# A second buffer for the tile of new node features, in the third and fourth node stages of a four-layer graph network

## The chip, the cores and the metric

The kernel runs on one core of one Trainium2 chip. The time is the device time of one execution, in microseconds (us); several executions are timed and their median is given.

## What is computed

A graph of 6250 nodes with 128 features each and 100,000 edges, sorted by destination, goes through four layers. Each layer's result is added to its input and normalised:

```python
x = _layernorm(x + L0(x, src, dst))                      # gated differences over the edges
x = _layernorm(x + L1(x, src, dst, edge_weight))         # attention with 4 heads, each normalised
x = _layernorm(x + L2(x, edges, edge_attr_32))           # attention with 8 heads, then
                                                         #   x1 = _layer_norm(x + agg @ Wo + bo)
                                                         #   _layer_norm(x1 + gelu(x1 @ W1 + b1) @ W2 + b2)
x = _layernorm(x + L3(x, edges))                         # two attention layers with 4 heads
```

In L1 the sum over a node's edges is divided by its denominator, every head is normalised over its 32 features (`norm_feat`) and averaged with the same of the node's own projection. The attention layers need a softmax over the edges that enter a node, so every layer gathers a row per edge, weighs it, and sums by destination.

## The kernel before, in words

The nodes lie on 128 partitions in 49 blocks (NB), and a node stage works through them in KG = 7 groups of KB = 7 blocks, so one pass over a group is 128 x 896 elements. The program alternates: node stage `ph` (0 to 5) builds new features of all nodes and the tables for the next edge loop; edge loop `ph` (0 to 4) gathers table rows for 56 groups of edges and leaves sums by destination in DRAM; the next node stage gathers those. Stage `ph` = 2 is the third node stage, `ph` = 3 the fourth. All order between engines is written out by hand with semaphores; each engine runs its own list of instructions in order. `link` and `tell` issue one DVE instruction and wait for it, so DVE has one pass in flight at a time, and many of its operations carry the line of a helper: L1281 is `tensor_tensor`, L1285 `tensor_scalar`, L1289 a copy, L1292 `scalar_tensor_tensor`, L1295 a reduction.

**Third stage.** DVE runs `features(0)`, then for each g `features(g+1)` and `tables(g)`. `features(g)` (L1849) takes the gathered sums of group g, divides, normalises each head (`norm`, L1593), scales, adds the kept own part `aux` and the old features X, all in the tile `t1` (a part of `rows`, called f1 there; f2 is scratch), and takes the statistics (`centre`, L1576). It has asked ACT for two square roots on the way (L1075). ACT then centres the seven blocks of t1 (L1088, semaphore n_x), PE turns them (L741, n_t), ACT copies the turned tile from PSUM to xT (L1064, L1065, n_xT) and copies t1 into X (L1144, n_kept); PE multiplies xT with the weights (L910, L913, n_mm). `tables(g)` (L1909) adds biases in three passes from PSUM (L1281) and counts n_stage. SyncE (SP) then saves the table (L550, L552), and GpSimd (POOL) scatters the rows of the group to the edges (`spread_rows`, L660). POOL also gathers the sums for the groups to come (`gather_sums`, L652); its list holds the gathers of three groups, then a gather and a scatter by turns. Before it writes t1, `features` waits for the turn and for the copy into X of the group before it (L1854 to L1857).

**Fourth stage.** A group passes through `head` (divide, into t1), `project` on PE (turn t1, multiply with Wo), `inner` on DVE (add X, statistics, in x1s[g % 2]), the feed-forward part on PE and ACT (turn x1 at L741, matrices at L870, gelu at L1159, second matrices at L882, n_ff2), `outer_first` on DVE (L1804: x1 times a gain into the tile yq, plus the second product from PSUM, statistics, a reciprocal root by three Newton steps on DVE, scaling), `outer_second` (L1831: gain, bias, plus X, statistics), ACT's centring of yq (L1088, y_ready), PE's `table_rows` (turn yq, matrices at L857 and L858), ACT's `keep` (L1146: copy to xT, copy yq into X at L1149, n_kept), and `tables`. DVE's round in this stage is outer_first(k-1), tables(k-2), outer_second(k-1), inner(k+1), head(k+2) (L1971 to L1981). PE's is: turn x1 of group k, L870, project(k+1), the second matrices, table_rows(k-1) (L864 to L885). `project(k)` waits from k = 3 on for the count that `tables(k-3)` gives. ACT's is: copy of the turned x1, eight gelus, copy for the projection, root and centring of outer_second(k-1), of inner(k+1), keep(k-1) (L1154 to L1168). The wait in question is the second line of `outer_first`, L1807: `dve.wait_ge(n_kept, kp.value())`, the copy of the group before.

yq is a part of `rows` (L157); `msg` (L94) is a tile of its own that DVE uses as scratch (f3) in the second node stage only, for the tables of that stage, and between edge loops for 132 columns.

## Time and profile before

| | us |
|---|---|
| three runs | 6608.78, 6615.19, 6615.32 |
| median | 6615.19 |
| the profiled execution | 6610.64 |
| its span, first to last instruction | 6608.9 |
| third node stage, about | 172 |
| fourth node stage, about | 245 |

The profile is of one execution, by the hardware's profiler. Engines are PE (TensorE), DVE (VectorE), ACT (ScalarE), POOL (GpSimd) and SP (SyncE); PEld is PE's load of weights. Over the whole span DVE is busy for 4656.9 us (70%), POOL for 4285.6 (65%), ACT for 1375.1 (21%) and PE for 1263.0 (19%). In a line of the timeline stand the start, the duration, the engine, the line of the code, the operation, what it writes and reads, the shapes and the count; in brackets the idle time of the engine before it and what ended that. Lines of the timeline can merge several instructions (x3).

### The profile page before, as it was taken

To read this page: it belongs to the slowest core of one execution; us is meant where nothing else is said; L and a number is where in the kernel's file an instruction comes from. 1 tells how busy PE (TensorE), PEld (TensorE's weight loads), DVE (VectorE), ACT (ScalarE), POOL (GpSimd) and SP (SyncE) were. 2 spreads that over 40 slices of the span, in tenths; PEclk is the share of its full clock that TensorE was granted. 3 is DMA by queue.
4 is the path that set the end of the run, shared out by engine and by line. 5 is a ranking of instruction groups with operands and counts; after the bars stand their busy time and mean duration, and the time that the engine had idled before them with its cause. 6 is when DMAs were issued, how large, how long until landed. Compare 5 with 4: busy or idle time off the path is not lost. (4 is left out here: it accounts for less than half of the span.)

```text
span 6608.9 us, 37159 instructions
## 1 busy us (share of the span) xinstructions
PE 1263.0 (19%) x8049; PEld 1103.2 (17%) x8049; DVE 4656.9 (70%) x9455; ACT 1375.1 (21%) x3580; POOL 4285.6 (65%) x4445
## 2 busy tenths in 40 slices
PE   7100000245555533332000000810000010000000
PEld 6100000135455433322000000610000010000000
DVE  7788888799999969976888887644444444444445
ACT  0122222221111114421000000622222211222223
POOL 1777777657777760026777775357777767777775
PEclk9555555555555555556555555855555555555555
DMA  9666666334444437744666664123333323333332
GB/s 386 208 213 202 202 203 203 123 105 132 136 134 135 133 130 295 294 155 139 218 224 215 224 218 157 29 75 112 111 109 115 109 79 91 109 115 109 110 113 82
DMA packets 338944, 1032.97 MB, mean 156 GB/s; under 512 B 100325, under 2 KB 163137, under 8 KB 331294
## 3 DMA queue, kind: packets, MB, share of 16 engines
q0 software_dynamic: 166752, 401.68, 21.3%
q1 hardware_dynamic: 116642, 342.34, 14.8%
q10 hardware_dynamic: 55324, 286.57, 12.0%
q8 instruction: 63, 1.03, 0.1%
q14 instruction: 163, 1.34, 0.1%
HBM read 602.97 MB, written 427.39 MB: 156 GB/s over the span
## 5 line engine op out<-in xcount | busy, mean ns | idle before, releaser
L722 POOL DMA_INDIRECT rows<-table,idx x3136 | 2988.0, 953 | 985.1 <-issue 972.9
L641 POOL DMA_INDIRECT by_src<-ebuf,place x784 | 764.9, 976 | 275.6 <-issue 239.0
L1292 DVE SCALAR_TENSOR_TENSOR psA<-psA,cont,dstf 128x128 f32<-128x128 f32 (+1 forms) x2349 | 836.6, 356 | 45.5 <-ACT ebuf L1021 24.8
L1281 DVE TENSOR_TENSOR sc<-rows,ebuf 128x56 f32<-128x56 f32 x112 | 28.2, 252 | 1023.6 <-DMA rows<-table,idx 1023.6
L954 PE MATMUL psA<-dstf,ones 128*128 128x512 f32 x10 | 9.9, 1114 | 3056.3 <-DVE dstf L2213 3056.3
L1292 DVE SCALAR_TENSOR_TENSOR sums<-sums,cont,psA 128x128 f32<-128x128 f32 (+1 forms) x1512 | 519.4, 344 | 30.2 <-ACT psA L1217 29.0
L954 PEld LDWEIGHTS psA<-dstf,ones 128*128 128x128 f32 x10 | 2.7, 316 | 3057.9 <-issue 3057.9
L820 PE MATMUL psA<-attr,sums 128*128 128x49 f32 x1568 | 406.1, 404 | 468.6 <-DVE attr L1471 468.6
L2094 DVE TENSOR_TENSOR_SCAN psA<-rows,psA 128x1980 f32<-128x1980 f32 x112 | 480.1, 4287 | 3.9
L820 PEld LDWEIGHTS psA<-attr,sums 128*128 128x128 f32 x1568 | 397.0, 327 | 474.7 <-DVE attr L1471 474.7
L1223 ACT ACTIVATE psA<-df 128x60 f32<-128x60 f32 (+1 forms) x168 | 40.4, 241 | 1716.0 <-DVE df L1281 1716.0
L1281 DVE TENSOR_TENSOR psA<-rows,psA 128x1848 f32<-128x1848 f32 (+1 forms) x168 | 352.9, 2101 | 0.0
L729 POOL DMA_INDIRECT fixr<-states,fixi x5 | 5.0, 997 | 518.3 <-DMA states<-sums 464.6
L660 POOL DMA_INDIRECT spread_wide<-rows,nidx x147 | 154.7, 1052 | 244.9 <-DMA spread_wide<-sums 143.9
L1281 DVE TENSOR_TENSOR rows<-rows,psA 128x1792 bf16<-128x1792 bf16 (+3 forms) x121 | 234.4, 1937 | 109.2 <-DMA rows<-table,idx 105.6
L652 POOL DMA_INDIRECT sums<-states,nidx x245 | 255.8, 1044 | 81.0 <-issue 73.1
L1238 ACT ACTIVATE sums<-psA 128x1848 f32<-128x1848 f32 x112 | 191.5, 1710 | 460.0 <-DVE psA L2094 460.0
L1281 DVE TENSOR_TENSOR rows<-psA,rows 128x1792 f32<-128x1792 f32 (+2 forms) x168 | 203.3, 1211 | 118.3 <-DMA rows<-table,idx 106.7
L1019 ACT ACTIVATE ebuf<-psA 128x1792 f32<-128x1792 f32 x56 | 94.2, 1681 | 902.4 <-DMA by_src<-ebuf,place 782.6
L792 PE MATMUL psA<-ebuf 128*128 128x49 bf16 x588 | 63.6, 276 | 963.4 <-DVE ebuf L1281 963.4
L1217 ACT ACTIVATE psA<-rows,wt 128x128 f32<-128x128 f32 x784 | 233.0, 352 | 33.8 <-DVE wt L2114 33.8
L792 PEld LDWEIGHTS psA<-ebuf 128*128 128x128 bf16 x588 | 54.5, 144 | 972.4 <-DVE ebuf L1281 972.4
(337 smaller groups left out, 5556.0 us busy)
## 6 DMA issues: line engine op xcount, KB each, us to landing
dstf<-spread_wide SPq DMA_DIRECT2D x168, 924.0 KB
states<-sums ACTq DMA_DIRECT2D x150, 952.0 KB, 4.0
rows<-by_src SPq DMA_DIRECT2D x55, 1035.0 KB, 5.1
states<-sums ACTq DMA_DIRECT2D x56, 1008.0 KB, 5.9
spread_wide<-sums SPq DMA_DIRECT2D x56, 924.0 KB, 24.7
states<-sums ACTq DMA_DIRECT2D x56, 903.0 KB, 7.3
rows<-table,idx POOLq DMA_INDIRECT x3136
msg<-low_rows SPq DMA_DIRECT2D x56, 448.0 KB, 3.7
```

The costliest lines, as they stand in the source:

```text
L641: pool.indirect_dma_start(by_src[:, :], bass.IndirectOffsetOnAxis(ap=place[:, s, j:j + 1], axis=0), payload[:, s, j, :], None).then_inc(so ...
L652: pool.indirect_dma_start(nrows[g % NS][:, b * w:(b + 1) * w], None, states[ph - 1][:, :], bass.IndirectOffsetOnAxis(ap=nidx[:, order, k:k ...
L660: pool.indirect_dma_start(spread[ph][:, :], bass.IndirectOffsetOnAxis(ap=nidx[:, 1, k:k + 1], axis=0), zslot(ph, g)[:, b * ZW[ph]:(b + 1) ...
L722: pool.indirect_dma_start(rows[:, at:at + GW[ph]], None, table[ph][:, :], bass.IndirectOffsetOnAxis(ap=idx[:, s, j:j + 1], axis=0)).then_i ...
L792: m = pe.matmul(cells, hotS[:, :, j], hotSH[:, :, j], start=False, stop=True, skip_group_check=True)
L820: pe.matmul(t, hotT[s][:, j, :], cell[:, :, j], start=True, stop=False)
L1019: act.activation(payload[:, s, :, 0:ROW].rearrange("p b (h d) -> p b h d", d=33)[:, :, :, 0:32], heldS[:, :, 0:D].rearrange("p b (h d) -> ...
L1217: m = act.activation(gated[:, j * D:(j + 1) * D], rows[:, at:at + D], ACT.Copy, scale=wt[:, s, j:j + 1])
L1238: act.activation(S3[:, :, 0:F], chain_msg.rearrange("p (f b) -> p b f", b=B + 1)[:, 1:B + 1, :], ACT.Copy).then_inc(states_turned, 1)
L1281: return dve.tensor_tensor(o_, a_, b_, op)
L1292: return dve.scalar_tensor_tensor(o_, a_, s_, b_, op0, op1)
L2094: tell(dve.tensor_tensor_scan(chain_msg, chain_gate, chain_msg, 0.0, ALU.mult, ALU.add), su)
```

## The change

In the third stage groups of even number are built in t1 as before, those of odd number in f3, a view of `msg`; in the fourth the same with yq and f3. Every reader follows: DVE's passes, ACT's centring and its copy into X, PE's turn. The waits of DVE in front of a group's first write are moved back by one group: in the third stage group 1 has none, and group g from 2 on waits for the turn and the copy of group g - 2; in the fourth `outer_first(g)` waits for the copy of group g - 2. A local name in `outer_first` is changed to make room (y becomes r), which alters no instruction; those lines are left out.

```diff
--- before.py
+++ after.py
@@ -156,6 +156,9 @@
         x1s = [t2, rows[:, o:o + KB * P].rearrange("p (b d) -> p b d", d=P)]
         yq = rows[:, o + KB * P:o + 2 * KB * P].rearrange("p (b d) -> p b d", d=P)
         mixed = [t1, yq]
+        f3 = msg[:, 0:KB * D].rearrange("p (b d) -> p b d", d=D)
+        fresh = [t1[:, :, 0:D], f3]
+        yqs = [yq, f3]
         dflat = dstf[:, :, :, :].rearrange("p s b d -> p (s b d)")
         hT = dflat[:, 0:4 * KB * P].rearrange("p (c n) -> p c n", c=4)
         sflat = small[:, :, :].rearrange("p a b -> p (a b)")
@@ -848,7 +851,7 @@
 
                 def table_rows(k):
 
-                    turn_x(yq, y_ready, k + 1)
+                    turn_x(yqs[k % 2], y_ready, k + 1)
                     if k < KG - 2:
                         pe.wait_ge(proj_read, k + 3)
                     if k:
@@ -898,7 +901,8 @@
                     if ph:
                         x.add()
                         pe.wait_ge(n_x, x.value())
-                    turn(KB, lambda b: t1[:, b, 0:D] if ph else X[:, g * KB + b, :]).then_inc(n_t, 1)
+                    entry = fresh[g % 2] if ph == 2 else t1
+                    turn(KB, lambda b: entry[:, b, 0:D] if ph else X[:, g * KB + b, :]).then_inc(n_t, 1)
                     xt.add()
                     pe.wait_ge(n_xT, xt.value())
                     w = 256 if ph < 3 else 136
@@ -1096,7 +1100,7 @@
                 def outer_second(k):
 
                     root(1, KB, 0)
-                    centre(2 * KG + 2 * k + 2 - int(k == KG - 1), yq, y_ready)
+                    centre(2 * KG + 2 * k + 2 - int(k == KG - 1), yqs[k % 2], y_ready)
 
                 def evict(g):
 
@@ -1125,7 +1129,7 @@
                     if ph == 2:
                         root(1, 28, 1)
                         root(1, KB, 0)
-                        centre(KG + g, t1, n_x)
+                        centre(KG + g, fresh[g % 2], n_x)
                     if ph == 4:
                         turned(ACT.Relu)
                         if g < KG - 1:
@@ -1141,12 +1145,12 @@
                     if ph in (0, 1, 2):
                         turned()
                     if ph in (1, 2):
-                        act.activation(X[:, grp(g), :], t1[:, :, 0:D], ACT.Copy).then_inc(n_kept, 1)
+                        act.activation(X[:, grp(g), :], fresh[g % 2] if ph == 2 else t1[:, :, 0:D], ACT.Copy).then_inc(n_kept, 1)
 
                 def keep(g):
 
                     turned()
-                    act.activation(X[:, grp(g), :], yq, ACT.Copy).then_inc(n_kept, 1)
+                    act.activation(X[:, grp(g), :], yqs[g % 2], ACT.Copy).then_inc(n_kept, 1)
 
                 if ph == 3:
                     turned()
@@ -1543,7 +1547,6 @@
             opn = Steps(n_open)
             f1 = t1[:, :, 0:D]
             f2 = t2[:, :, 0:D]
-            f3 = msg[:, 0:KB * D].rearrange("p (b d) -> p b d", d=D)
             tn = Steps(n_t)
             kp = Steps(n_kept)
 
@@ -1803,37 +1806,39 @@
 
                 def outer_first(g):
 
+                    y = yqs[g % 2]
                     dve.wait_ge(x1_ready, g + 1)
-                    dve.wait_ge(n_kept, kp.value())
-                    link(tt(yq, x1s[g % 2], bcol("L2_gnn_ln1_g"), ALU.mult))
+                    dve.wait_ge(n_kept, kp.value() - min(g, 1))
+                    link(tt(y, x1s[g % 2], bcol("L2_gnn_ln1_g"), ALU.mult))
                     ff2.add()
                     dve.wait_ge(n_ff2, ff2.value())
-                    tell(tt(yq, yq, mmX, ALU.add), fr)
+                    tell(tt(y, y, mmX, ALU.add), fr)
                     for b in range(KB):
-                        m = dve.bn_stats(halves[:, b, :], yq[:, b, :])
+                        m = dve.bn_stats(halves[:, b, :], y[:, b, :])
                     link(m)
                     for b in range(KB):
                         m = dve.bn_aggr(spreadv[:, b, :], halves[:, b, :])
                     link(m)
-                    v, y, q, m0 = (small[:, 8, 14 + KB * k:14 + KB * (k + 1)] for k in range(4))
+                    v, r, q, m0 = (small[:, 8, 14 + KB * k:14 + KB * (k + 1)] for k in range(4))
...
                     for b in range(KB):
-                        m = ts(yq[:, b, :], yq[:, b, :], y[:, b:b + 1], ALU.mult, m0[:, b:b + 1], ALU.add)
+                        m = ts(y[:, b, :], y[:, b, :], r[:, b:b + 1], ALU.mult, m0[:, b:b + 1], ALU.add)
                     link(m)
 
                 def outer_second(g):
 
-                    link(tt(yq, yq, bcol("L2_gnn_ln2_g"), ALU.mult))
-                    link(tt(yq, yq, bcol("L2_gnn_ln2_b"), ALU.add))
-                    link(tt(yq, yq, X[:, grp(g), :], ALU.add))
-                    spread_of(yq)
+                    y = yqs[g % 2]
+                    link(tt(y, y, bcol("L2_gnn_ln2_g"), ALU.mult))
+                    link(tt(y, y, bcol("L2_gnn_ln2_b"), ALU.add))
+                    link(tt(y, y, X[:, grp(g), :], ALU.add))
+                    spread_of(y)
                     kp.add()
 
                 def ask_exponentials(g):
@@ -1851,9 +1856,13 @@
                     Xg = X[:, grp(g), :]
                     Ag = aux[:, grp(g), 0:D]
 
-                    if not first and ph < 5:
+                    if ph == 2 and not first:
+                        if g >= 2:
+                            dve.wait_ge(n_t, tn.value() - 1)
+                            dve.wait_ge(n_kept, kp.value() - 1)
+                    elif not first and ph < 5:
                         dve.wait_ge(n_t, tn.value())
-                    if ph in (1, 2) and not first or ph in (2, 4) and first:
+                    if ph == 1 and not first or ph in (2, 4) and first:
                         dve.wait_ge(n_kept, kp.value())
                     kp.add(int(ph in (1, 2)))
                     tn.add(XS[ph])
@@ -1868,14 +1877,15 @@
                         centre(f1)
                     if ph == 2:
                         Rh = h4(R[:, :, 0:F], 4)
+                        fa = fresh[g % 2]
                         link(ts(sm(2, 4), Rh[:, :, :, 32], 1e-10, ALU.max))
                         link(dve.reciprocal(sm(2, 4), sm(2, 4)))
-                        tell(tt(h4(f1, 4), Rh[:, :, :, 0:32], sm(2, 4).unsqueeze(3).to_broadcast([P, KB, 4, 32]), ALU.mult), usd)
-                        norm(f1, f2, 4, f1)
-                        link(tt(f1, f1, bcol("scale0"), ALU.mult))
-                        link(tt(f1, f1, Ag, ALU.add))
-                        link(tt(f1, f1, Xg, ALU.add))
-                        centre(f1)
+                        tell(tt(h4(fa, 4), Rh[:, :, :, 0:32], sm(2, 4).unsqueeze(3).to_broadcast([P, KB, 4, 32]), ALU.mult), usd)
+                        norm(fa, f2, 4, fa)
+                        link(tt(fa, fa, bcol("scale0"), ALU.mult))
+                        link(tt(fa, fa, Ag, ALU.add))
+                        link(tt(fa, fa, Xg, ALU.add))
+                        centre(fa)
                     if ph in (4, 5):
 
                         Rh = h4(R[:, :, 0:F], 4)
```

## Rows read from the trace of the kernel before

**Rows 1.** The page's first line: span and instructions

```profile
span 6608.9 us, 37159 instructions
```

**Rows 2.** Windows of both stages: length, busy PE, PEld, DVE, ACT, POOL, clock, DMA

```profile
2903.00:3075.00 172.00, 61.14 (x245) 51.48 (x245) 115.93 (x228) 38.12 (x87) 94.88 (x92) 0.64 0.30 87
4108.00:4353.00 245.00, 174.28 (x1036) 134.02 (x1036) 155.39 (x575) 124.15 (x235) 92.60 (x92) 0.81 0.12 29
```

**Rows 3.** Waits of DVE, third stage: us in total, times, longest

```profile
DVE small L1285 <- ACT X L1144: 23.8, 6, 6.6
```

**Rows 4.** Waits of DVE, fourth stage

```profile
DVE rows L1281 <- ACT X L1149: 22.9, 6, 5.8
```

**Rows 5.** Timeline of DVE, third stage: start, duration, instruction, [idle before it]

```profile
2930.81 0.17 DVE L1292 SCALAR_TENSOR_TENSOR small<-small 128x7 f32<-128x7 f32 x1
2937.56 0.20 DVE L1285 TENSOR_SCALAR small<-sums 128x28 f32<-128x28 f32 x1 [6.59 <-ACT X L1144]
...
2951.97 3.34 DVE L1281 TENSOR_TENSOR rows<-psA,bias 128x896 f32<-128x896 f32 x3
2958.75 0.20 DVE L1285 TENSOR_SCALAR small<-sums 128x28 f32<-128x28 f32 x1 [3.44 <-ACT X L1144]
...
3043.59 0.20 DVE L1285 TENSOR_SCALAR small<-sums 128x28 f32<-128x28 f32 x1 [3.44 <-ACT X L1144]
```

**Rows 6.** Timeline of ACT, third stage, group 0

```profile
2931.01 2.80 ACT L1088 ACTIVATE rows<-rows,small 128x128 f32<-128x128 f32 x7 [0.47 <-DVE small L1292]
...
2936.52 0.95 ACT L1144 ACTIVATE X<-rows 128x896 f32<-128x896 f32 x1
```

**Rows 7.** POOL by line, third stage: busy us, mean ns, idle before

```profile
L652 POOL DMA_INDIRECT sums<-states,nidx x49 | 51.2, 1045 | 16.2 <-issue 14.6 <-DMA states<-fixr,fixi 1.6
L660 POOL DMA_INDIRECT spread_wide<-rows,nidx x42 | 42.7, 1017 | 55.9 <-DVE rows L1281 44.9 <-issue 11.0
```

**Rows 8.** DVE by form, third stage

```profile
L1281 DVE TENSOR_TENSOR rows<-rows,X 128x896 f32<-128x896 f32 x7 | 7.6, 1092 | 0.2
```

**Rows 9.** DMA issues, 2950 to 3080 us: KB each, us to landing

```profile
table<-rows SPq DMA_DIRECT2D x7, 924.0 KB, 4.2
```

**Rows 10.** Tile msg in the second stage: ns min/median/max

```profile
L1281 DVE TENSOR_TENSOR msg<-msg,small x14: 1091/1093/1126, 1294.9 to 1400.2; 128x896 f32<-128x896 f32 x14
```

**Rows 11.** Timeline of DVE, fourth stage, starts of outer_first

```profile
4182.26 1.09 DVE L1281 TENSOR_TENSOR rows<-rows,bias 128x896 f32<-128x896 f32 x1 [2.75 <-ACT X L1149]
...
4209.14 1.09 DVE L1281 TENSOR_TENSOR rows<-rows,bias 128x896 f32<-128x896 f32 x1 [2.71 <-ACT X L1149]
...
4295.51 1.09 DVE L1281 TENSOR_TENSOR rows<-rows,bias 128x896 f32<-128x896 f32 x1 [5.38 <-ACT X L1149]
...
4319.62 1.09 DVE L1281 TENSOR_TENSOR rows<-rows,bias 128x896 f32<-128x896 f32 x1 [5.83 <-ACT X L1149]
```

**Rows 12.** Timeline of PE, fourth stage

```profile
4159.51 0.98 PE L741 MATMUL psA<-ident,rows 128*128 128x128 f32 x7 [0.26 <-ACT rows L1088]
...
4184.50 0.96 PE L741 MATMUL psA<-ident,rows 128*128 128x128 f32 x7
...
4208.22 0.49 PE L857 MATMUL psA<-WA,rows 128*128 128x128 f32 x2 [2.22 <-ACT rows L1065]
...
4297.77 0.96 PE L741 MATMUL psA<-ident,rows 128*128 128x128 f32 x7
...
4307.73 6.52 PE L882 MATMUL psA<-W,dstf 128*128 128x128 f32 x56 [0.33 <-ACT dstf L1159]
...
4323.88 0.78 PE L857 MATMUL psA<-WA,rows 128*128 128x128 f32 x2
```

**Rows 13.** Windows of two rounds of the fourth stage

```profile
4182.00:4210.00 28.00, 22.89 (x158) 17.69 (x158) 23.05 (x83) 17.54 (x34) 11.59 (x12) 0.99 0.12 28
4210.00:4238.00 28.00, 24.80 (x145) 18.88 (x144) 21.26 (x82) 17.61 (x33) 15.41 (x15) 0.83 0.17 40
```

**Rows 14.** Waits of DVE, edge loop behind the third stage

```profile
DVE rows L1281 <- DMA rows<-table,idx: 96.3, 39, 7.9
```

More of the change, by code:

```diff
@@ L1817, in outer_first @@
                     link(m)
-                    v, y, q, m0 = (small[:, 8, 14 + KB * k:14 + KB * (k + 1)] for k in range(4))
+                    v, r, q, m0 = (small[:, 8, 14 + KB * k:14 + KB * (k + 1)] for k in range(4))
                     link(ts(v, spreadv[:, :, 1], 1e-5, ALU.add))
-                    link(ts(y.bitcast(I32), v.bitcast(I32), 1, ALU.arith_shift_right))
-                    link(ts(y.bitcast(I32), y.bitcast(I32), -1.0, ALU.mult, float(0x5f3759df), ALU.add))
+                    link(ts(r.bitcast(I32), v.bitcast(I32), 1, ALU.arith_shift_right))
+                    link(ts(r.bitcast(I32), r.bitcast(I32), -1.0, ALU.mult, float(0x5f3759df), ALU.add))
                     for _ in range(3):
-                        link(tt(q, y, y, ALU.mult))
+                        link(tt(q, r, r, ALU.mult))
                         link(stt(q, q, -0.5, v, ALU.mult, ALU.mult))
-                        link(stt(y, q, 1.5, y, ALU.add, ALU.mult))
-                    link(stt(m0, spreadv[:, :, 0], -1.0, y, ALU.mult, ALU.mult))
+                        link(stt(r, q, 1.5, r, ALU.add, ALU.mult))
+                    link(stt(m0, spreadv[:, :, 0], -1.0, r, ALU.mult, ALU.mult))
                     for b in range(KB):
-                        m = ts(yq[:, b, :], yq[:, b, :], y[:, b:b + 1], ALU.mult, m0[:, b:b + 1], ALU.add)
+                        m = ts(y[:, b, :], y[:, b, :], r[:, b:b + 1], ALU.mult, m0[:, b:b + 1], ALU.add)
                     link(m)
                 def outer_second(g):
-                    link(tt(yq, yq, bcol("L2_gnn_ln2_g"), ALU.mult))
-                    link(tt(yq, yq, bcol("L2_gnn_ln2_b"), ALU.add))
-                    link(tt(yq, yq, X[:, grp(g), :], ALU.add))
-                    spread_of(yq)
+                    y = yqs[g % 2]
[3 more added lines that the diff above has]
+                    spread_of(y)
                     kp.add()
```

## The prediction

> **What bounds the kernel now.** The measured time is one core's, and the page gives its span as 6608.9 us [rows 1]; that execution took 6610.64 us, so 1.7 us lie around the span. The first view to read is the table of windows, cut at the two stages that the change touches. The third node stage takes 172 us of which VectorE (DVE) works 115.9; the fourth takes 245 us, with PE at 174.3 and DVE at 155.4 [rows 2]. So DVE leads the third stage and is not full; in the fourth no engine is full, and the chain between them sets the time. The second view is the list of waits. In the third stage DVE waits 23.8 us, six times, for ScalarE's (ACT's) copy of the features into X at L1144 [rows 3]; in the fourth 22.9 us, six times, for the same copy at L1149 [rows 4]. Both are the wait on n_kept: the next group may not write the tile (t1, or yq) until ACT has centred it, PE has turned it and ACT has copied it. The third view is the timeline, where one asks of each such wait what is late next. Each node stage lies between two edge loops that need all of its output, so a microsecond off a stage's end is one off the span.
>
> **The third stage.** One round of DVE is features(g+1), then tables(g). Group 0 shows the bare chain: DVE's last instruction is at 2930.81, ACT centres from 2931.01 for 2.80 us, copies into X from 2936.52 for 0.95, and DVE, idle for 6.59 us, starts group 1 at 2937.56 [rows 5, 6]. From then on tables, 3.34 us in three passes, hides half of it: the idle time is 3.44 us in front of groups 2 to 6 [rows 5] (five rows alike, of which the first and the last stand there). The sum 6.59 + 5 x 3.44 = 23.8 is that of the waits.
> With two tiles features(g) waits only for the turn and the copy of group g-2, which ended a whole round ago. Group 1 starts at once, and a round shrinks from (3043.59 - 2958.75) / 4 = 21.21 us to 21.21 - 3.44 = 17.77. What could be late next:
> - ACT. It still has 0.95 us of the copy to do at 2936.52, so until 2937.47, when DVE, moved up, asks for its first square root some 6.4 us into group 1 (a reading of the timeline: two small instructions, four passes of 1.09 and two small ones), at 2937.4. That is at most 0.1 us, once. In later rounds tables lies between, and ACT has 3.3 us to spare.
> - POOL. It issues seven gathers (51.2 + 14.6 us for seven groups, 9.4 each) and seven scatters (42.7 + 11.0 for six, 8.95 each) [rows 7], 18.35 us a round, which is more than 17.77. But only four rounds carry both, the last three carry scatters alone. The first scatter can start at 2949.5 (tables(0) ends 6.6 us before its 2955.31), and the gather for group 6, behind three scatters and two gathers, is issued by 2949.5 + 3 x 18.35 = 3004.6 and needed at 3043.59 - 23.8 = 3019.8. Of the 4 x 0.58 us by which POOL falls behind, the rounds without gathers give all back before the last scatter. Cost: nothing; the cover is 15 us for the gathers, less 2 or 3 for landing.
> - The save of the table, which must have left the staging tile before tables writes it again: it lands in 4.2 us [rows 9], the next write comes 14.4 us after its issue.
> - The other tile. Three groups of seven now live in msg. DVE passes of the same 896 columns on msg took 1.093 us in the second stage [rows 10], against 1.092 on rows here [rows 8]: nothing.
> After features(6) the order is as before (centre, turn, matrices, tables(6), scatter), so the whole shift reaches the end. Third stage: 23.8 - 0.1 = **23.7 us**.
> Passes now run beside more of POOL's and ACT's work. The group-0 passes run beside gathers today, and the mean over seven groups is 1.092 us [rows 8], so I cost that at nothing. The Trainium skill, page "SBUF — State Buffer", section "Who interferes with whom", says that a DVE instruction with two SBUF inputs contends with a GpSimd instruction that reads SBUF, and that whoever comes second is blocked. If DVE were the one held, for one POOL instruction of about 1 us in each of seven such passes a group, the stage would lose 7 us a round where it gains 3.44, some 25 us on balance; the trace does not bear it out.
>
> **The fourth stage.** PE's round goes from one turn of x1 to the next. The one that nothing disturbs is 4159.51 to 4184.50, 24.99 us [rows 12]. DVE's round, from one outer_first to the next, is 4209.14 - 4182.26 = 26.88, of which 2.71 is the wait on the copy: 24.17 of its own [rows 11]. Today the two are tied in a ring: outer_first waits for keep, keep for PE's turn of yq, and that turn stands behind project, which needs the stage count that tables gives only after outer_first. The four rounds of PE from 4184.50 to 4297.77 take 113.27 us, 13.3 more than 4 x 24.99: PE waits 2.22 us for ACT, which is late with centring [rows 12], and in every second round the granted clock falls, 0.83 of full against 0.99 [rows 13].
> With two tiles the ring is open. outer_first needs x1_ready, long given, and in its second instruction n_ff2, which PE gives about 5 us before each turn of x1 and so about 2.7 us before keep lets DVE go. DVE, 24.17 a round, then follows PE, 24.99 a round, and tables ends some 3 us before project wants its count. So PE's chain with ACT is what is late next, and the turn of group 6's x1 comes at 4184.50 + 4 x 24.99 = 4284.46, 13.3 us earlier. The last rounds are shorter (no projection, no head), and DVE waits 5.38 and 5.83 us there [rows 11]. The second matrix product of group 6 ends at 4307.73 + 6.52 = 4314.25 [rows 12], 16.48 after that turn; in the new order at 4300.94. DVE is there in time: it starts outer_first(5) at about 4278.5 and its round is 4319.62 - 4295.51 - 5.83 = 18.28 [rows 11]. So its second instruction, at 4320.75 before, comes at 4301.0: 19.7 us earlier. Of that 0 to 0.6 us may go to PE's product for the table of group 5, whose last block begins at 4323.88 [rows 12] at the lower clock, 7.2 us after its turn. The tail behind it keeps its order. Fourth stage: **19.4 us**.
> No instruction is added, no DMA moves to another queue, and the first group of each stage waits as before. The wait on n_kept stays in the code, one group later: behind it stand the whole of outer_first and features, but what it waits for is then a round old.
>
> **The sum.** 23.7 + 19.4 = 43.1 us; 6610.64 - 43.1 = 6567.5 for the profiled execution. The median of the three runs, 6615.19, lies 4.6 above it, which would give 6572.1. I say **6570**, and for this case alone 6563 to 6577. The edge loop behind the third stage starts in the same order, only earlier.
>
> **The rivals.**
> - The clock keeps falling. PE's round has three gaps of about 1 us even when undisturbed, and nobody has shown that 24.99 holds four times in a row; one round in two runs at 0.83 today [rows 13]. If all the 13.3 us of losses stay with PE, the fourth stage gains only 19.7 - 13.3 = 6.4, in all 30.1 us: 6580.5 to 6585, about 6583. For it: the falls follow gaps that partly remain. Against it: the undisturbed rounds with gaps near 1 us hold 0.99. Were the clock to fall in all four rounds, at 6.7 each, the stage would lose 6.9 us, for 6594 in all. The Trainium skill, page "TensorE: Matmul & The Clock Gate", section "A second HAM failure mode: psum-queue depth-cycling", tells of a kernel whose engine idles in small gaps between groups of matmuls often enough that its clock swings; by that rule this rival is the forecast, by the row of the window at 0.99 it is not.
> - Another wait takes the place in the fourth stage, so that only the third gains: 6610.64 - 23.7 = 6586.9, about 6589. It would need ACT to be the late one; ACT works 124 of 245 us [rows 2], which speaks against it.
> - The change doesn't do what it says (a remaining wait stands in front of the same copy): 6611 to 6615. Speaks for it nothing but that the waits are counted.
> - Slower: the edge loop behind the third stage gives back more than is won. In it DVE waits 96.3 us in 39 waits for gathered rows to land [rows 14], with 56 groups in which gathers and stores of states share the DMA engines. If the earlier start sets the two against each other, so that each group waits 1.0 us more, it costs 56 us and the kernel ends at 6623 to 6628; from 43.1 / 56 = 0.77 us a group on the sign turns. Against it: gathers, stores and loads start in the same order with the same distances as before, since all follow the last table.
>
> **How the numbers follow.** Forecast 0.76; clock 0.11; only the third stage 0.05; no effect 0.04; slower 0.04. The range reaches from 6560 (the forecast with up to 3 us more, if the first products of the last group of the third stage start at a higher clock after a shorter gap) to 6589, which takes in the clock rival and stops at the third. A difference of 0.2%, 13 us, is about what a measurement of this kernel can tell from no change. Faster 0.92, same 0.04, slower 0.04.
>
> **What would show it.** In the third stage DVE's waits for L1144's copy are gone and a round is 17.8 us; the last scatter starts 23.7 us earlier after the stage's first gather. In the fourth DVE's waits for the copy at L1149 are gone, PE's turns of x1 are 25.0 apart at a clock near 0.99, and some of DVE's idle time now stands in front of the sum with PE's second product, above all in group 6. I am wrong if the rounds stay at 21.2 or 26.9, if the granted clock of the fourth stage does not rise above 0.81 [rows 2], or if the edge loop grows.

## The result, and the profile after

Five runs of each kernel gave a median of 6577.24 us (6569.18 to 6581.19) after and 6615.32 us (6608.78 to 6617.22) before, a ratio of 0.9938 (95% interval 0.9928 to 0.9949): 38 us, or 0.6%, faster. The forecast of 6570 was 7 us too low, and the range of 6560 to 6589 holds the time. The profiled execution took 6572.1 us; its page begins:

```profile
span 6570.3 us, 37158 instructions
PE 1251.3 (19%) x8049; PEld 1094.3 (17%) x8049; DVE 4654.6 (71%) x9455; ACT 1375.2 (21%) x3580; POOL 4293.2 (65%) x4445
```

The span is 38.6 us shorter than that of [rows 1]. To see where they lie I cut both spans at the same instructions: a stage runs from the start of its first reciprocal of the gathered denominators to the start of its last 128-column product with the table matrices (us):

| | before | after | change |
|---|---|---|---|
| up to the third stage | 2916.7 | 2919.8 | +3.1 |
| third stage | 154.4 | 129.6 | -24.8 |
| edge loop between | 1050.1 | 1049.1 | -1.0 |
| fourth stage | 227.9 | 212.0 | -15.9 |
| the rest | 2259.8 | 2259.8 | 0.0 |

The first row is work that the change does not touch, and in the runs below it varies from 2918.8 to 2922.5. The forecast was -23.7 and -19.4 for the two stages.

**Third stage.** Below are DVE's waits from just before it to its end, which answer [rows 3]; the third of them lies ahead of the stage (in the kernel after, the lines touched here stand 3 or 4 further down: L1144 is L1148, L741 is L744, L882 is L885):

```profile
DVE small L1289 <- DMA sums<-states,nidx: 12.7, 1, 12.7
DVE rows L1285 <- PE psA L917: 9.0, 1, 9.0
DVE msg L1285 <- PE psA L966: 4.1, 1, 4.1
DVE small L1605 <- ACT small L1079: 2.7, 7, 0.4
DVE small L1593 <- ACT small L1079: 2.6, 7, 0.4
```

The 23.8 us for ACT's copy are gone, and no wait of that size has come in their place. The timeline of DVE shows the three passes of each `tables`:

```profile
2966.28 3.34 DVE L1285 TENSOR_TENSOR rows<-psA,bias 128x896 f32<-128x896 f32 x3
2984.07 3.34 DVE L1285 TENSOR_TENSOR rows<-psA,bias 128x896 f32<-128x896 f32 x3
...
3037.45 3.34 DVE L1285 TENSOR_TENSOR rows<-psA,bias 128x896 f32<-128x896 f32 x3
3049.80 3.34 DVE L1285 TENSOR_TENSOR rows<-psA,bias 128x896 f32<-128x896 f32 x3 [9.02 <-PE psA L917]
```

From 2966.28 to 3037.45 are four rounds of 17.79 us; the forecast said 17.77, and [rows 5] had 21.21. POOL, whose work of 18.35 us a round is longer than that, shows first no gap and then these, in front of the last three scatters:

```profile
3023.76 1.79 POOL L663 DMA_INDIRECT spread_wide<-rows,nidx  x1 [3.50 <-DVE rows L1285]
...
3041.56 0.97 POOL L663 DMA_INDIRECT spread_wide<-rows,nidx  x1 [8.17 <-DVE rows L1285]
...
3053.92 0.97 POOL L663 DMA_INDIRECT spread_wide<-rows,nidx  x1 [3.73 <-DVE rows L1285]
```

It fell behind, caught up when its gathers were done, and waits for DVE again at the end: the stage ends with DVE and PE, as before.

**Fourth stage.** DVE's waits from just before it until its last 0.5 us, against [rows 4]; those for L966 and L958 lie ahead of the stage:

```profile
DVE rows L1285 <- PE psA L849: 23.7, 2, 17.5
DVE small L1289 <- DMA sums<-states,nidx: 12.9, 1, 12.9
DVE small L1593 <- ACT small L1079: 11.8, 14, 5.2
DVE msg L1285 <- PE psA L966: 7.5, 1, 7.5
DVE dstf L1285 <- PE psA L958: 3.9, 1, 3.9
DVE rows L1285 <- PE psA L885: 3.3, 1, 3.3
DVE msg L1285 <- PE psA L885: 1.8, 1, 1.8
```

The 22.9 us for L1149's copy are gone. The two last rows are what the prediction asked for, waits for the second product, 3.3 of them in the last group. But the wait for ACT's root (the square root that DVE asks of ACT) has one case of 5.2 us, which was not foreseen. PE's turns of x1 show why; they start at 4136.72, 4161.71, 4186.68, 4212.68, 4240.59 and 4265.56, and the windows between them (length, then busy time and count of PE, PEld, DVE, ACT and POOL, granted clock, DMA share, GB/s) are:

```profile
4136.70:4161.70 25.00, 21.60 (x149) 16.65 (x150) 22.97 (x96) 17.46 (x33) 0.00 (x0) 1.00 0.00 1
4161.70:4186.70 25.00, 21.62 (x153) 16.66 (x151) 22.75 (x86) 17.52 (x33) 13.50 (x13) 1.00 0.16 37
4186.70:4212.70 26.00, 22.62 (x153) 17.67 (x151) 23.00 (x88) 17.53 (x33) 14.79 (x15) 0.96 0.19 46
4212.70:4240.60 27.90, 24.69 (x151) 18.34 (x151) 21.27 (x78) 17.61 (x33) 7.05 (x7) 0.86 0.09 20
4240.60:4265.60 25.00, 21.62 (x153) 16.66 (x152) 20.48 (x81) 17.53 (x33) 7.03 (x7) 1.00 0.10 22
```

Three of the five last 24.97 or 24.99 us, as forecast. The other two, 26.00 and 27.91, share one fall of the clock, across the border between them:

```profile
4208.50 0.49 PE L860 MATMUL psA<-WA,rows 128*128 128x128 f32 x2 [1.07 <-ACT rows L1069]
...
4211.83 0.77 PE L860 MATMUL psA<-WA,rows 128*128 128x128 f32 x2
...
4212.68 1.73 PE L744 MATMUL psA<-ident,rows 128*128 128x128 f32 x7
4215.49 9.36 PE L873 MATMUL psA<-rows,W 128*128 128x448 f32 x16 [1.07 <-ACT rows L1069]
4225.08 0.94 PE L744 MATMUL psA<-ident,rows 128*128 128x128 f32 x7
```

The same pair of matmuls takes 0.49 and then 0.77 us, the turn 1.73 where it took 0.96 in the round before, and the sixteen matmuls of L873 take 9.36 where they took 1.77 + 5.26 with 0.18 between. That is 1.2 GHz in place of 2.4, from about 4210.5 until the middle of L873. PE's last gap before it is the usual one of 1.07 us. Behind the fall DVE stands 5.17 us in front of a root.

### The profile page after: what moved, and what is told of

It reads as the page before. It is cut to its first block and busy times, and to the rows that moved or that the text cites. A ratio compares the mean times of both kernels' runs of the same rounds, so it can differ in the third digit from the quotient of the medians.

```text
span 6570.3 us, 37158 instructions
## 1 busy us (share of the span) xinstructions
PE 1251.3 (19%) x8049; PEld 1094.3 (17%) x8049; DVE 4654.6 (71%) x9455; ACT 1375.2 (21%) x3580; POOL 4293.2 (65%) x4445
## 3 DMA queue, kind: packets, MB, share of 16 engines
q10 hardware_dynamic: 55324, 286.57, 12.1%
## 5 line engine op out<-in xcount | busy, mean ns | idle before, releaser
L958 PE MATMUL psA<-dstf,ones 128*128 128x512 f32 x10 | 9.9, 1113 | 3055.3 <-DVE dstf L2223 3055.3
L958 PEld LDWEIGHTS psA<-dstf,ones 128*128 128x128 f32 x10 | 2.7, 317 | 3056.9 <-issue 3056.9
```

## The experiments

Three theories (the sections and the recorded expectations refer to them by letter) were left after the result. **A**: the forecast's own, in which PE's chain with ACT bounds the fourth stage once the ring is open, and what is missing from 19.4 us is one fall of the clock. **B**: DVE, or its passes on the other tile, is the new bound, so that the missing microseconds are DVE's. **C**: the gain belongs to the second tile and not to the moved wait, or one stage's gain depends on the other's.

The eight runs of the next two sections fell on another chip, on which every kernel run there is slower: the kernel before takes 7607.2 us (35 runs, 7562 to 7635) and 7608.6 in the second batch (35 runs, 7571 to 7653). They can be compared with each other only. Runs of one kernel scatter there by 0.5%, so the length of the stages, cut as above, says more than the ratio.

### One stage at a time

```diff
-        yqs = [yq, f3]
+        yqs = [yq, yq]
...
-                    dve.wait_ge(n_kept, kp.value() - min(g, 1))
+                    dve.wait_ge(n_kept, kp.value())
```

> The change in the third node stage alone; the fourth is as before. Theory A (each stage gains by itself): the third stage is 24 to 25 us shorter, its rounds 17.8 us, the fourth as long as before with its six waits of DVE for the copy into X (22.9 us); total 0.37% below the kernel before, near 6590 us. Rival B (the stages share something, such as an edge loop that shortens or lengthens with the start): the total differs from 24 us by more than 5.

> The change in the third stage alone, once more, since the chip of the first look was disturbed. Theory A: third stage 129 to 130 us where it was 154.4 (from the first reciprocal to the last matrix), fourth 228, total 24 to 26 us below the kernel before.

And the fourth stage alone, with `fresh = [t1[:, :, 0:D], t1[:, :, 0:D]]` and the old waits in `features`:

> The change in the fourth node stage alone. Theory A: PE's turns of x1 come 24.99 us apart save where the granted clock falls; the stage is 16 to 20 us shorter, near 6597 us in all. Theory A2 (the single fall of the clock seen in the changed kernel is a matter of chance): it is in another round here, or absent, and the stage is then 19.5 us shorter. Rival B: less than 10 us, because the third stage's shift had a part in it.

> The change in the fourth stage alone, once more. Theory A: third stage 154.4 us, fourth 208 us if the granted clock holds in all rounds (turns of x1 24.97 us apart), 212 with one fall of it; total 16 to 20 us below the kernel before. Rival: the fall comes in every execution, 212 us.

### The tiles with the old waits, and the change itself

In the third kernel both tiles alternate, but each wait is the old one, for the group before. The fourth is the changed kernel once more.

> Both tiles alternate, but DVE waits for the copy of the group just before, as in the kernel before. Theory A (the gain is the wait alone, and a tile in msg costs nothing): same time as before within 3 us, rounds of 21.2 us in the third stage, waits of 23.8 and 22.9 us. Rival (where the tile lies matters for DVE, ACT or PE): passes on msg differ from 1.09 us and the stage lengths move.

> Both tiles alternate and the old waits stand, once more. Theory A: as the kernel before within 3 us, third stage 154.4 us, fourth 228. Rival (the second tile itself costs or gains): another stage length and other durations of the passes on msg.

> The changed kernel once more. It tells what a second execution repeats: theory A2 (the clock's fall in the fourth stage is chance): another round or none has it, and the stage's length differs by about 4 us. Rival: the same fall between the third and the fourth turn of x1, so that it belongs to the schedule. The 3 us by which the part before the third stage was later in the changed kernel's profile should not repeat, if it is chance.

> The changed kernel on the same chip as the single parts. Theory A: the total is the sum of the two parts within 3 us; the fourth stage is 208 or 212 us, with the clock's fall at another round than before or absent. Rival: the fall again between the third and the fifth turn of x1, 212 us.

Measured, two profiles and two sets of runs of each:

| on the slower chip | ratio to the kernel before (interval) | third stage | fourth stage |
|---|---|---|---|
| third stage only | 0.9989 (0.9966 to 1.0012), 0.9964 (0.9940 to 0.9989) | 137.9, 142.9 | 269.8, 269.2 |
| fourth stage only | 0.9992 (0.9967 to 1.0018), 0.9969 (0.9944 to 0.9995) | 154.2, 153.3 | 251.6, 250.1 |
| tiles, old waits | 0.9972 (0.9949 to 0.9995), 0.9996 (0.9967 to 1.0025) | 153.2, 154.4 | 261.0, 264.5 |
| the change | 0.9957 (0.9935 to 0.9980), 0.9956 (0.9933 to 0.9979) | 136.7, 139.2 | 253.4, 246.1 |

With the tiles alternating and the old waits, the second run's list of DVE's waits in the third stage has again

```profile
DVE small L1289 <- ACT X L1148: 23.8, 6, 6.6
```

so the gain there belongs to the moved wait; the tile alone does nothing there (153.2 and 154.4, against 154.2 and 153.3 with t1 only), which is also the price of `msg` in that stage: none that can be seen. Each stage's gain comes without the other's. Where the third stage changes it is 137.9, 142.9, 136.7 and 139.2, a mean of 139.2, against 153.8: 14.6 us. The fourth is 250.3 on average in the four profiles that change it, against 269.5 in the two that leave it alone: 19.2. The sum, 33.8 us, is 0.44% of 7607, and the two ratios of the whole change are 0.9957 and 0.9956. That agreement proves little: the edge loop between the stages took anything from 1282.9 to 1313.9 us in these eight profiles, a scatter of 31 us, and the intervals of the single parts overlap with those of the tiles with the old waits. The stage lengths carry the argument. In the third stage theory C falls.

In the fourth one thing is not clean: the tiles with the old waits gave 262.8 us, some 7 less than the old stage with one tile. The moved wait is not what they gained: DVE still waits 38.8 and 44.5 us there for ACT's copy at L1153, against 42.0 and 43.6 with one tile, and with the moved wait these waits are gone. Some 3 of the 7 us lie in the last two rounds between turns of x1, where the granted clock was 1.00 in both these runs, and 0.83 and 0.85, then 0.85 and 1.00, in the two of the third stage alone; whether that is a coincidence of four profiles I can't say. What does not depend on it is the stretch from the turn of group 6's x1 to the end of the stage: 46.1 to 46.4 us in the four profiles with the moved wait, 52.1 to 52.5 in the four without, whatever the tile. So the fourth stage gains from the moved wait too; that all 19.2 us come from it is not shown.

Two things on this chip were not expected. The first is that the third stage gains 14.6 us and not 24.8. In all four profiles with the new wait there, DVE stalls once in front of a `tables`, the third of seven or, in one of them, the fourth. None of the four profiles with the old wait has it, nor any on the other chips:

```profile
3512.16 3.34 DVE L1285 TENSOR_TENSOR rows<-psA,bias 128x896 f32<-128x896 f32 x3 [7.64 <-remote]
3530.02 3.34 DVE L1285 TENSOR_TENSOR rows<-psA,bias 128x896 f32<-128x896 f32 x3
```

This is the change once more; in the three others the stall is 6.27, 7.78 and 9.47 us, and all four end between 3511 and 3520 us of the span. The trace names no releaser that ran on the core, and ACT's copy of the next turn stalls in the same stretch though PE's turn before it had ended at 3509.16:

```profile
3507.41 1.75 PE L744 MATMUL psA<-ident,msg 128*128 128x128 f32 x7 [8.73 <-ACT msg L1092]
3513.61 0.60 ACT L1068 ACTIVATE rows<-psA 128x512 f32<-128x512 f32 x1 [6.25 <-remote]
```

What it is stays open. It is not POOL, which issues gathers without a gap through it, and a late landing of the table's save, which could hold DVE, would by the code not hold ACT's copy.

The second is in the fourth stage, where the two rounds behind the third turn of x1 last 36.39 and 35.14 us in that profile (40.59 and 40.61 in the second run of the third stage alone), and no kernel here has them shorter than 35 on that chip. Part of PE's 56 matmuls of the second product go out one by one there:

```profile
4957.25 0.27 PE L885 MATMUL psA<-W,dstf 128*128 128x128 f32 x1 [0.84 <-issue]
4957.98 0.27 PE L885 MATMUL psA<-W,dstf 128*128 128x128 f32 x1 [0.46 <-issue]
4958.69 0.37 PE L885 MATMUL psA<-W,dstf 128*128 128x128 f32 x1 [0.44 <-issue]
```

In these rows a matmul comes about every 0.7 us with nothing to wait for that the profile shows, and the whole product takes 16.3 us (12.1 to 18.0 in these two rounds of the eight profiles). On the first chip it takes 6.5 us. This is there with and without the change.

### Half a pass more of DVE

If B holds, more work on DVE lengthens every round of the fourth stage; if A holds, it vanishes in them. The runs from here on fell on a chip like the first (the kernel before: 6611.29 us, nine runs, 6608.9 to 6615.91).

```diff
                         link(tt(fa, fa, Xg, ALU.add))
+                        link(tt(f2[:, 0:4, :], fa[:, 0:4, :], Xg[:, 0:4, :], ALU.add))
                         centre(fa)
...
                     link(tt(y, y, X[:, grp(g), :], ALU.add))
+                    link(tt(spare, y[:, 0:4, :], X[:, bass.ds(g * KB, 4), :], ALU.add))
```

> The changed kernel with one more DVE pass over four of seven blocks (512 columns, some 0.65 us) in each group of the third stage and in each outer_second of the fourth; it reads what the stage has just written and writes a spare place. Theory A (DVE is late next in the third stage, PE's chain with ACT in the fourth): the third stage grows by 7 x 0.65 = 4.5 us, PE's turns of x1 in the fourth stay 24.97 us apart where the clock holds, and that stage grows by less than 1.5 us, at its last groups. Rival B (DVE is the bound of both): 4.5 us in the fourth too, turns 25.6 apart.

Measured, in a single run: 6577.38 us. The third stage took 134.8 us, 5.2 more than 129.6, where DVE is the bound. The fourth took **208.5**, which is no more than 212.0 but less. Its five rounds between the turns of x1 of groups 1 to 6 are 25.66, 24.97, 24.97, 24.97 and 24.96 us, and two of the windows read

```profile
4194.30:4219.30 25.00, 21.62 (x153) 16.67 (x151) 22.96 (x84) 17.53 (x33) 15.12 (x15) 1.00 0.19 43
4219.30:4244.20 24.90, 21.52 (x150) 16.57 (x151) 22.86 (x84) 17.54 (x33) 8.96 (x9) 1.00 0.13 31
```

DVE's extra work, about 0.7 us a round by the third stage (5.2 / 7), costs nothing in the last four rounds, so B falls for them. It shows in full at both ends: the first round is 25.66 us where it was 24.99, since ACT, which waits for DVE, centres some 0.7 us later and so hands PE its copy that much later:

```profile
4166.19 0.49 PE L861 MATMUL psA<-WA,rows 128*128 128x128 f32 x2 [1.74 <-ACT rows L1070]
```

(the gap is 1.07 in the changed kernel), and the stretch behind the turn of group 6's x1 is 45.92 us where it was 45.24. In the first round, then, DVE's chain through ACT has no slack. And in this run the clock did not fall in any of the five rounds: from the turn of group 2 to that of group 6 it took 99.87 us, against the 4 x 24.99 = 99.96 of the forecast. That the whole stage comes to 227.9 - 19.4 = 208.5 to the digit is chance, since 0.67 and 0.68 us of the pass and 0.8 less in group 0 (22.55 us for 23.36, at a clock of 0.85 for 0.82) are in it. This is one profile, and I do not read the missing fall as an effect of the pass.

### Work for PE in two of its gaps

PE waits 1.07 us for ACT's copy behind each turn. Four matmuls of the identity, written to a piece of PSUM that is overwritten before anything reads it, fill that gap behind the turns of x1 and yq.

```diff
                     turn(KB, lambda b: tile[:, b, 0:D]).then_inc(n_t, 1)
+                    for _ in range(4 if fill else 0):
+                        pe.matmul(psM[:, 2, 0:P], ident[:, :], ident[:, :], start=True, stop=True)
                     xt.add()
```

> The changed kernel with four idle 128x128 matmuls of the identity behind each turn of x1 and of yq in the fourth stage, in the gap of 1.07 us in which PE waits for ACT's copy. Theory A (what is missing of the forecast is the clock's fall, and the fall follows the gaps): no fall in the rounds between turns of x1, all 25 us apart, the stage about 4 us shorter than in the changed kernel (208 us from the first reciprocal to the last matrix for the table, where it was 212.0). Rival: the clock falls all the same, once or more, and the stage is 212 us or longer, since the added matmuls also can delay the next.

Measured: 6565.56 us (four runs, 6564.6 to 6571.4), a ratio of 0.9930 (0.9915 to 0.9945). The ratio's interval overlaps with that of the change alone (0.9928 to 0.9949), so a gain of the whole kernel over the changed one is not shown; the stage shows more. The fourth stage took 205.2 us, 6.8 less than after the change. The first of the windows is that of group 0, from its turn of x1 to the next, which the changed kernel ran in 23.36 us at a clock of 0.82:

```profile
4118.08:4139.88 21.80, 20.48 (x123) 15.42 (x123) 6.21 (x22) 12.70 (x22) 15.12 (x16) 0.90 0.24 59
4139.88:4164.87 24.99, 23.40 (x166) 18.54 (x166) 22.95 (x96) 17.47 (x33) 0.00 (x0) 1.00 0.00 1
...
4214.80:4239.77 24.97, 23.38 (x169) 18.52 (x167) 22.14 (x83) 17.54 (x33) 7.06 (x7) 1.00 0.11 24
```

```profile
4140.70 1.06 PE L839 MATMUL psA<-ident 128*128 128x128 f32 x8
4141.93 0.64 PE L875 MATMUL psA<-rows,W 128*128 128x448 f32 x1 [0.17 <-ACT rows L1071]
```

The gap in front of the first matrices is 0.17 where it was 1.07, and all five rounds behind the first take 24.96 to 24.99 us at a clock of 1.00. That is no faster than an undisturbed round without the filling: PE waits for ACT's copy all the same, and only its idle time is filled. So the 6.8 us fall into three parts. The four rounds from the turn of group 2 to that of group 6 take 99.87 us for 103.85, which is the missing fall, 4.0 us; the half pass had 99.87 too, without any filling. Group 0 takes 21.80 for 23.36, 1.6 us; but with the filling of the last section below it takes 22.39, and with the half pass and no filling 22.55. And the stretch behind the last turn of x1 takes 43.92 for 45.24, 1.3 us. There the clock comes back in the middle of the last table's matrices, which without the filling run at 1.2 GHz to the end; the first row below is the changed kernel's, the second this one's:

```profile
4310.16 0.77 PE L860 MATMUL psA<-WA,rows 128*128 128x128 f32 x2
```

```profile
4308.32 0.47 PE L862 MATMUL psA<-WA,rows 128*128 128x128 f32 x2
```

Both profiles with the filling have this return of the clock, and none of the three without it on these chips after the change. At 1.2 GHz the filling also has a price: the four matmuls last 1.9 us, longer than the gap, and the first product starts 3.26 us after its turn instead of 2.82.

Whether filling prevents the falls in the later rounds is not shown. The two profiles with it have none; of three without it two have one, and those two have it at the same place: the clock falls at 4210.5 us in the changed kernel and at 4210.1 in the one of the next section, 97 us after the first turn of x1 in both. In the kernel before, the first fall in these rounds came 97 us after that turn too (4209.5). So where the clock falls looks tied to the schedule and not to chance (three profiles, and no run that tests it), and what keeps it up with the half pass or the filling is open. The Trainium skill, page "TensorE: Matmul & The Clock Gate", section "A second HAM failure mode: psum-queue depth-cycling", says that frequent small idle gaps between groups of matmuls can make the clock swing. By that rule the gaps of 1.07 us, three in every round, would bring it down; yet the rounds of 24.97 us at 1.00 have the same gaps, so they alone do not decide when it falls.

### Fetching the gelu's table early

In the changed kernel ACT loads a table of functions between its copy and the first gelu of each group:

```profile
4188.17 0.48 ACT L1069 ACTIVATE rows<-psA 128x384 f32<-128x384 f32 x1
4188.68 1.28 ACT L1163 ACT_TABLE_LOAD   x1
4189.97 1.18 ACT L1163 ACTIVATE dstf<-psA,b1c 128x448 f32<-128x448 f32 x2
```

A gelu of one element, issued behind `inner(0)` and behind each `keep`, moves the load into the time in which ACT waits for PE.

```diff
+                def fetch_gelu():
+
+                    act.activation(small[:, 11, 8:9], eps[:, 0:1], ACT.Gelu)
...
                             keep(k - 1)
+                        if k < KG - 1:
+                            fetch_gelu()
```

> The changed kernel with one small gelu on ACT before it waits for PE's turn of x1, so that the table of functions is loaded in that wait. Theory A (PE's chain with ACT sets the fourth stage's round, and the 1.28 us table load stands in it): turns of x1 24.3 us apart instead of 24.97, since DVE's own round of 24.2 comes next; five rounds give 3 to 4 us. Rival B (DVE or another wait sets the round): no change. Rival C (a copy between evicts the table): one more load each round, up to 1.3 us longer.

Measured: 6571.69 us (five runs, 6569.24 to 6577.12), 0.9942 (0.9928 to 0.9955); fourth stage 211.1, 0.9 less. That is a miss of mine, since I had asked for 3 to 4 us. The clock fell here as in the changed kernel (rounds of 25.67 and 28.04 us). The load did move, but the gelu did not follow it:

```profile
4189.39 1.39 ACT L1168 ACTIVATE dstf<-psA,b1c 128x448 f32<-128x448 f32 x2 [1.11 <-PE psA L873]
```

It now waits 1.11 us for PE's first product, which has needed the same copy all the time, and starts 3.09 us after the turn of x1 (at 4186.30) where it started 3.29 after it (at 4186.68). The load had lain beside PE's product and was worth 0.2 us a round, 24.77 for 24.97. The Trainium skill, page "ScalarE: Activation LUTs", section "What ACT_TABLE_LOAD costs", gives 2.66 us for a switch, 1.28 of it the load and the rest a drain. The load agrees to the digit; no drain is to be seen, since the copy ends at 4188.65 and the gelu begins at 4189.97. The rows decide.

### Both

> The changed kernel with the early gelu and the filled gaps together. Theory A: the fourth stage about 7 us shorter than in the changed kernel (205 us where it was 212.0), the kernel some 45 us below the kernel before. Rival: what the one gives takes the other away, because filled gaps delay the turns that the early gelu has moved up; then no better than the better of the two.

Measured: 6564.02 us (five runs, 6562.42 to 6565.14), 0.9927 (0.9914 to 0.9941), 47.3 us less than the kernel before, with a fourth stage of 204.0 us. This is the fastest kernel of the case. It is clearly faster than the kernel before; its median is 1.5 us under that of the filled gaps alone, whose runs overlap with it, so what the early table adds to the total is not shown. The clock is 1.00 in its last five rounds, which take 25.12 us and then four times 24.77, the same as the undisturbed rounds with the early table alone.

## Why the prediction was right, and where it was off

**The third stage held step by step.** The waits for the copy went, the round is 17.79 for 17.77, POOL fell behind and gave it all back, the passes on msg cost 1091 to 1092 ns like those on rows:

```profile
L1285 DVE TENSOR_TENSOR rows<-rows,X 128x896 f32<-128x896 f32 x4 | 4.4, 1092 | 0.1
L1285 DVE TENSOR_TENSOR msg<-msg,X 128x896 f32<-128x896 f32 x3 | 3.3, 1091 | 0.1
```

The gain was 24.8 us against 23.7. The 1.1 more is in the wait for PE's last product, 9.0 us where it was 10.1. That was the "up to 3 us more" at the lower end of the range, and the reason given there is near: PE had stood idle for 8.16 us ahead of its last turn where it was 12.11, and the clock came back 6.2 us after that turn's start instead of 8.4, though the first products still ran at 1.2 GHz. That a DVE pass with two SBUF inputs is held by POOL, which the prediction weighed, is not seen: the mean of seven such passes, with POOL at work without a gap beside most of the stage, is 1092 ns.

**The fourth stage had the right bound, and one term of its sum was mis-sized.** PE with ACT took over from the ring, at 24.97 us a round where nothing disturbs it, and DVE follows in the last four of the five rounds with 0.7 us to spare, as the half pass shows; in the first it has nothing to spare. The term "4 x 24.99" for the four rounds from the turn of group 2's x1 to that of group 6 was 99.96 us; it measured 4265.56 - 4161.71 = 103.85. The 3.9 us are the two rounds across the one fall of the clock. The last part was right: from the turn of group 6's x1 to the end of its second product are 4282.04 - 4265.56 = 16.48 us again, and the end of the stage came another 6.4 us closer to that turn (19.7 - 13.3 in the prediction). 19.4 - 3.9 is 15.5, and 15.9 was measured.

**The rival of the clock was neither right nor wrong.** I had priced it at all or nothing: no fall, all the 13.3 us of losses kept, or a fall in each of the four rounds at 6.7 us, a price for which I gave no row; the one fall cost 3.9. It came where before there was some loss in each of four rounds, and the same kernel on a like chip, with half a pass more on DVE, had none. A better sum would have given the falls a number between 0 and 4 at some 4 us each, with a middle forecast between 6572 (none) and 6576 (one). Before, the clock fell twice in these rounds (at 4209.5 and 4264.1 us); after, once. The ring's own waits are gone, and with them the longer gaps of PE such as the 2.22 us of [rows 12], but that this is the reason is argued and not shown: the fall that is left comes 97 us after the first turn of x1 as the first one did, now behind gaps of 1.07 us only. What brings the clock down was not found.

**The other rivals fall.** Both stages gained, so it is neither one alone nor a change without effect. The edge loop behind the third stage, priced at up to 56 us, took 1049.1 us for 1050.1, and the waits for gathered rows from the end of the third stage to the fourth are the same in both kernels, before first:

```profile
DVE rows L1281 <- DMA rows<-table,idx: 105.6, 40, 9.2
```

```profile
DVE rows L1285 <- DMA rows<-table,idx: 104.3, 40, 9.5
```

(The window is a little wider than that of [rows 14].)

**What does not follow from the argument** is the slower chip: 14.6 us in the third stage instead of 24.8, for a stall that no step of it contains. The sign and the order of size hold there too.

## What to carry to other kernels

A wait for a consumer that repeats in front of every group is worth its idle time only down to the next ring. Write down the own round of every engine in the stage (here 17.77 against POOL's 18.35, and 24.17 against PE's 24.99), and count in how many rounds the longer one really applies. Where the next bound is PE with small gaps, its round has two lengths, at either clock; price each fall, and do not expect cheap work in PE's gaps to shorten a round that already runs at full clock. Eight idle matmuls a round left it at 24.97 us; what they may give is the clock after an idle stretch, 1.3 us at the end of the stage here, and the falls that they may prevent, 4 us here, if it was they. Before moving an instruction off a chain, ask what else its successor waits for: the table load of 1.28 us was worth 0.2.

## What the runs showed of the hardware

- The granted clock fell from 2.4 to 1.2 GHz and came back inside the fourth stage: in the third and fourth of five rounds in the changed kernel (0.96 and 0.86) and, 0.4 us earlier in the span, in the same kernel with the early table (0.96 and 0.85); in none of the five with half a pass more on DVE or with filled gaps; and at 0.83 and 0.84 in the second and third on the slower chip. The gaps of PE ahead of it, of 1.07 us, are the same in rounds with and without a fall.
- DVE passes with two SBUF inputs (128x896, fp32) took 1091 to 1092 ns with POOL issuing indirect DMAs beside them.
- Two chips ran the same program at 6611 and 7608 us. On the slower one the part before the third stage took 3417 to 3449 us instead of 2917 to 2923, PE's matmuls in one stretch came 0.7 us apart with no wait shown, and one stall of DVE and ACT at once appears only at the quicker pace of the third stage. Its cause is open.
